# A second home for the mixer's mixed rows, and a layer norm moved within the mixer's loop

## The reference

```python
x = x + 0.5 * ffn(layernorm(x))        # shared expert + one of 8 routed experts per token
x = x + mixer(layernorm(x))
x = x + 0.5 * ffn(layernorm(x))

def mixer(x):
    u = x @ W_in + b_in                 # 256 -> 512 channels
    u = causal_conv4(u) + conv_b        # depthwise, 4 taps
    # per channel: h = tanh(A) h + u_t Bp ; y_t = Cp . h + D u_t   (16 states)
    y = silu(ssm(u))
    return y @ W_out + b_out            # 512 -> 256

def ffn(x):                             # swiglu: silu(x wg) * (x wu) @ wd
    return swiglu(x, shared) + swiglu(x * score, expert[argmax(x @ gate_w)])
```

## Time and profile before

| | |
|---|---|
| median of 3 runs | 890.16 us (887.72 to 890.94) |
| span of the profiled execution | 884.5 us |
| PE busy | 830.2 us, 94% of the span |
| VectorE busy | 489.0 us, 55% |
| ScalarE busy | 390.7 us, 44% |
| POOL busy | 459.1 us, 52% |
| mean granted TensorE clock | 0.991 of full |

### The profile page before, as it was taken

One profiled execution on the slowest core, in us unless ns is written; L12 is line 12 of the kernel. 1 busy time (PEld: TensorE's weight loads), 2 busy tenths in 40 slices (PEclk: granted clock), 3 DMA queues, 4 the chain that ended last, 5 costly groups with the idle time before them and its releaser, 6 DMA issues.

```text
span 884.5 us, 16195 instructions
## 1 busy us (share of the span) xinstructions
PE 830.2 (94%) x5302; PEld 720.8 (81%) x5303; DVE 489.0 (55%) x999; ACT 390.7 (44%) x766; POOL 459.1 (52%) x435
## 2 busy tenths in 40 slices
PE   5889999999999999989998999899999999999993
PEld 4677888888888878877887888688888888888883
DVE  7877843333333336678998886975433333333452
ACT  5633323334343434555786776223343434344330
POOL 6527850333334018869999982686330242330685
PEclk9999999999999999999999999999999999999997
DMA  7683443545564225331010014154335555421566
GB/s 262 241 326 104 170 161 114 202 174 213 167 218 157 74 88 80 43 44 17 13 54 26 25 50 191 48 183 179 110 127 194 197 194 195 167 89 30 108 155 154
DMA packets 52917, 118.15 MB, mean 134 GB/s; under 512 B 6426, under 2 KB 41380, under 8 KB 48516
## 3 DMA queue, kind: packets, MB, share of 16 engines
q0 software_dynamic: 17536, 74.33, 27.1%
q1 hardware_dynamic: 34834, 43.15, 14.8%
q10 hardware_dynamic: 498, 0.02, 0.0%
HBM read 83.25 MB, written 34.22 MB: 133 GB/s over the span
## 4 chain that ended last, share of the span: by engine, by line
PE 70%; POOL 13%; DVE 8%; issue 3%; DMA 3%; ACT 2%; POOLq 0%; DVEq 0%; ACTq 0%
PE bank L419 21%; PE bank L420 20%; PE bank L421 20%; POOL acc L1888 5%; PE bank L616 4%; DMA wr_hi<-w_routed 2%; PE bank L585 2%; POOL v L1791 2%; DVE v L1503 2%; POOL wr_lo L1858 1%; POOL yr L1997 1%; DVE xT_lo L1194 1%; PE bank L486 1%; POOL hT_lo L1795 1%; DMA xT_kept<-xTf_odd 1%
## 5 line engine op out<-in xcount | busy, mean ns | idle before, releaser
L1858 POOL TENSOR_TENSOR wr_lo<-wr_raw,wr_hi 128x3072 fp32r<-128x3072 f32 x14 | 95.4, 6812 | 105.3 <-DMA wr_hi<-w_routed 87.0
L419 PE MATMUL bank<-wr_hi,xT_hi 128*128 x312 | 130.1, 417 | 1.5 <-POOL wr_lo L1858 1.4
L420 PE MATMUL bank<-wr_hi,xT_lo 128*128 x312 | 123.8, 397 | 0.0
L421 PE MATMUL bank<-wr_lo,xT_hi 128*128 x312 | 122.9, 394 | 0.0
L1461 DVE TENSOR_TENSOR hf<-sg,bank 128x512 f32<-128x512 f32 x78 | 53.6, 688 | 125.2 <-PE bank L421 125.2
L1194 DVE TENSOR_TENSOR hT_lo<-bank,hT_hi 128x512 fp32r<-128x512 f32 x78 | 53.9, 691 | 124.6 <-ACT hT_hi L869 124.6
L1888 POOL DMA_INDIRECT acc<-ys_sorted,pos x52 | 84.7, 1628 | 54.3 <-DMA ys_sorted<-rows 39.9
L419 PE MATMUL bank<-xT_hi,ws_hi 128*128 128x512 f32 x256 | 103.1, 403 | 8.0 <-DVE hf L1299 5.5
L420 PE MATMUL bank<-xT_hi,ws_lo 128*128 128x512 f32 x256 | 101.3, 396 | 0.0
L421 PE MATMUL bank<-xT_lo,ws_hi 128*128 128x512 f32 x256 | 101.2, 395 | 0.0
L419 PE MATMUL bank<-wr_hi,hT_hi 128*128 x312 | 93.8, 300 | 3.0 <-DVE hT_lo L1194 3.0
(11 more groups left out here) (245 smaller groups left out, 2117.6 us busy)
## 6 DMA issues: line engine op xcount, KB each, us to landing
wr_raw<-w_routed POOLq DMA_DIRECT2D x16, 1536.0 KB, 7.0
wr_hi<-w_routed POOLq DMA_DIRECT2D x16, 1536.0 KB, 7.7
rows<-xs_sorted SPq DMA_DIRECT2D x78, 128.0 KB, 2.5
ys_sorted<-rows SPq DMA_DIRECT2D x78, 128.0 KB, 1.7
xg<-xT_kept SPq DMA_DIRECT2D x12, 512.0 KB, 5.5
xT_kept<-xTf SPq DMA_DIRECT2D x9, 512.0 KB, 2.6
acc<-x SPq DMA_DIRECT2D x8, 512.0 KB, 9.8
xs_sorted<-zeros POOLq DMA_DIRECT2D x4, 1024.0 KB, 11.6
```

The lines of the kernel that those rows point to most:

```text
L419: pe.matmul(o, a_hi, b_hi, start=start, stop=False, skip_group_check=True)
L420: pe.matmul(o, a_lo, b_hi, start=False, stop=False, skip_group_check=True)
L421: return pe.matmul(o, a_hi, b_lo, start=False, stop=stop, skip_group_check=True)
L1858: pool.tensor_tensor(wr_lo[:, e % 2, :], wr_raw[:, :], f32(wr_hi[:, e % 2, :]), ALU.subtract).then_inc(s_wl, 1)
```

## The change

Two tiles `xM_hi` and `xM_lo` are laid in the place of `rows`. `mix_hi`, `mix_lo` and `w_in_part` use them for odd groups and `xT_hi`, `xT_lo` for even ones; `mix_hi(n)` waits for the `w_in_part`s of group n-2 (for n = 1: for the stores of the routed rows of the first half). On ScalarE `ln2_apply(n+2)` moves from the middle of iteration n to its end, just ahead of `ln2_hi(n+2)`. On VectorE `ln2_stats(n+2)` moves from ahead of `taps(n-1, 2)` to behind `ln2_lo(n+1)`. POOL's and SyncE's programs stay as they are.

```diff
+        mixer_only = ExitStack()
+        xM_hi = sb("xM_hi", [P, KB, GN], F32R, mixer_only)
+        xM_lo = sb("xM_lo", [P, KB, GN], F32R, mixer_only)
+        mixer_only.close()
         rows = sb("rows", [P, 2 * GT, H], F32)
...
+        def mixed(n): return (xT_hi, xT_lo) if n % 2 == 0 else (xM_hi, xM_lo)
...
+                m_hi, m_lo = mixed(n)
                 for kb in range(KB):
-                    mm = mm3(pe, UB[cb % 2][:, :], win_hi[:, kb, cs], win_lo[:, kb, cs], xT_hi[:, kb, :],
-                             xT_lo[:, kb, :], start=(kb == 0), stop=(kb == KB - 1))
+                    mm = mm3(pe, UB[cb % 2][:, :], win_hi[:, kb, cs], win_lo[:, kb, cs], m_hi[:, kb, :],
+                             m_lo[:, kb, :], start=(kb == 0), stop=(kb == KB - 1))
...
             def mix_hi(n):
-                if n > 0:
-                    act.wait_ge(s_um, 4 * n)
+                if n == 1:
+                    for j in range(RING):
+                        act.wait_ge(s_yst[j], 16 * (NS // RING))
+                elif n > 1:
+                    act.wait_ge(s_um, 4 * (n - 1))
                 for kb in range(KB):
                     act.wait_ge(s_zp, KB * n + kb + 1)
-                    hi(xT_hi[:, kb, :], ZB[kb][:, :]).then_inc(s_zh, 1)
+                    hi(mixed(n)[0][:, kb, :], ZB[kb][:, :]).then_inc(s_zh, 1)
...
                     if live(n + 1):
                         state_hi(n + 1, 0)
-                    if live(n + 2):
-                        ln2_apply(n + 2)
                     if live(n - 1):
                         y_round(n - 1, 3)
...
                     if live(n - 2):
                         ln3_apply(n - 2)
                     if live(n + 2):
+                        ln2_apply(n + 2)
                         ln2_hi(n + 2)
...
-                    lo(xT_lo[:, kb, :], ZB[kb][:, :], xT_hi[:, kb, :]).then_inc(s_zl, 1)
+                    lo(mixed(n)[1][:, kb, :], ZB[kb][:, :], mixed(n)[0][:, kb, :]).then_inc(s_zl, 1)
...
                     if live(n - 3):
                         ln3_stats(n - 3)
-                    if live(n + 2) and n > 0:
-                        ln2_stats(n + 2)
                     if live(n - 1):
                         taps(n - 1, 2)
...
                     if live(n + 1) and n > 0:
                         ln2_lo(n + 1)
+                    if live(n + 2) and n > 0:
+                        ln2_stats(n + 2)
                     if live(n):
                         taps(n, 0)
                         taps(n, 1)
```

## The result

| | before | changed |
|---|---|---|
| median | 890.55 us (4 runs) | 911.39 us (4 runs) |
| ratio | 1 | 1.0245 (1.022 to 1.0269) |
| span of the profiled execution | 884.5 us | 908.6 us |
| mean granted TensorE clock | 0.991 | 0.987 |

A forecast was written before the change was run, and what follows sets the result against it. The prediction took POOL (GpSimd) to set the mixer loop's pace up to 480 us. Its terms, 0.6 + 5.8 + 3 x 4.7 less 0.6 us, gave +20 us on 890.16, so 910 us, range 902 to 919.

The forecast's parts named there:

- (a), the homes: Second home of the mixed rows: `mix_hi` waits less, pays once at the first handover, then PE's limit is `xl`.
- (b), the late apply: ScalarE's `ln2_apply` moved later: `ln2_lo` starts at t+9.6 instead of t+8.7, t being the start of `y_silu(n, 0)`.
- (c) and the sum: VectorE's `ln2_stats` moved behind `ln2_lo`: POOL waits at `ln2_rsqrt` anew each iteration; all parts total +20 us.
- up to t(1): Loop until `y_silu(1, 0)` starts: POOL's wait of 0 to 2.2 us, say 1.1, less 0.5 for collisions: +0.6 us.
- t(1) to t(2): From `y_silu(1, 0)` to `y_silu(2, 0)`: a stall of 6.8 us less 1.0 for collisions, +5.8 us.
- t(2) to t(5): From `y_silu(2, 0)` to `y_silu(5, 0)`: three iterations, each stretched 5.7 us less 1.0 for collisions, 3 x 4.7 us.
- given back behind t(5): After `y_silu(5, 0)` starts, PE takes over and `mix_chunk(7, 0)` can start relatively sooner; 0.6 us comes back.
- credit of 1 us per iteration: Taken off for n = 2 to 5, because a standing POOL no longer collides with `ln2_lo`: 1.0 us each.
- low bound of +15.4: Smallest loss: nothing at n = 1, statistics ending 1 us sooner each time, 4.9 + 3 x 3.7 - 0.6.
- Paid once: Rival: in the loop, work behind the stall catches up within the iteration; +5 to +13 us, 898 us, chance 0.10.
- Faster, and no change: Two rivals without POOL's stall: gaps close for -6 us, 884 us, chance 0.05; or nets out within 0.5%, chance 0.02.
- PE as the bound at the lower clock: Rival: in the loop, idle PE drops to half clock and becomes the bound; +28 to +45 us, 925 us, chance 0.07.

The follow-up runs named there:

- pool_busy: Kernel before with nothing moved, POOL filling an unused tile three times ahead of `ln2_rsqrt` in iterations 2 to 5; 906.8 us, ratio 1.0223.
- gather_only: Kernel before, one home, with two of the four gathers of group 3 set on POOL ahead of `add_bias(0, 0)`; 884.24 us, ratio 0.9955.
- homes_only: Changed kernel with `ln2_apply` and `ln2_stats` at their old places, so only the two homes of the mixed rows remain; 889.97 us, ratio 1.0016.
- front_loaded: Kernel before plus two homes, two gathers moved early, and `ln2_lo(1)`, `ln2_stats(3)`, `ln2_apply(2)` set ahead of the loop; 886.01 us, ratio 0.9968.
- front_one_home: `front_loaded` with a single home for the mixed rows; 885.53 us, ratio 0.9969.
- apply_back: Changed kernel with ScalarE's `ln2_apply(n+2)` put back behind `state_hi(n+1, 0)`; 907.7 us, ratio 1.0218.
- stats_back: Changed kernel with VectorE's `ln2_stats(n+2)` put back ahead of `taps(n-1, 2)`; 890.88 us, ratio 1.0026.
- one_late: Changed kernel with `ln2_stats(n+2)` late in iteration 2 alone and at its old place in the others; 896.23 us, ratio 1.0099.
- rsqrt_late: Changed kernel with POOL's `ln2_rsqrt(n+2)` moved behind `add_bias(n, 1)`; 893.26 us, ratio 1.0065.

## Why the prediction was right, point by point

**The bound.** POOL as the pace of the loop up to 480 us was the step that everything hung on. `pool_busy` and `gather_only` show it from both sides: 5.8 us of added POOL time per iteration cost 4.5 to 4.9 us each, and 3.55 us given back once moved t(5) by 3.65 us.

**(a), the homes.** Expected to pay only at the first handover and to run into `xl` there: `homes_only` is equal to before within its interval, and `front_loaded` against `front_one_home` shows the 0.9 us that two homes give at that gap and that none of it reaches the end.

**(b), the late apply.** `ln2_lo(4)`, ahead of the statistics that POOL waits for in iteration 3, was to start at t(2) + 9.6; it started at 449.66, t(2) + 9.74. Its share of the loop is what `apply_back` took away, 0.8 to 1.0 us in iterations 3 to 5 and nothing in iteration 2, as the sum has it. By itself (`stats_back`) it costs 2.3 us behind t(5). The sum had no term for that, and needed none while the stall was there: in the changed kernel `mix_chunk(7, 0)` starts at t(5) + 11.3, not + 14.6.

**(c) and the sum, term by term.** On the left is the forecast, on the right what the two traces show, with the 1.72 us by which the changed kernel's mixer starts late (386.49 against 384.77 us for the first instruction of the first `first_tap`) taken out. The row behind t(5) is read at the start of `mix_chunk(7, 0)`, 521.98 against 497.74 us:

| term | forecast | measured |
|---|---|---|
| up to t(1) | +0.6 | +2.2 |
| t(1) to t(2) | +5.8 | +6.1 |
| t(2) to t(5) | +14.1 | +14.6 |
| given back behind t(5) | -0.6 | -0.3 |
| sum | +20 (19.9) | +22.5 |
| outside the mixer | 0 | +1.7 |

The term that was mis-sized is the first. I had let `ln2_lo(2)` take 1.2 to 3.6 us and the wait 0 to 2.2; it took 4.34 us, and POOL waited 3.14 us. The collision there did not go away, it grew. The credit of 1 us per iteration for collisions that end was right: the `y_low` behind `ln2_rsqrt` took 1.30 us at 454.81 where the earlier trace rows had 2.35, and the steps grew by 4.8 to 4.9 us while POOL stood 6.04 to 6.06 us. The rule of the Trainium skill (SBUF — State Buffer, "Who interferes with whom"), that a VectorE instruction with two SBUF inputs and a GpSimd instruction that reads SBUF block each other, was weighed the right way here, except for the first term; how `ln2_lo(2)` came to wait so long is told below. The low bound of +15.4 has a slip, on which nothing hangs: for n = 2 `ln2_lo` had been taken at t + 8.7 already, so by its own terms it is 5.8 + 11.1 - 0.6 = +16.3.

The 1.7 us outside the mixer are a half-clock stretch that the profiled execution of the changed kernel has at about 50 us, where nothing was edited and the kernel before has none:

```profile
48.00:55.00 7.00, 5.81 (x47) 5.54 (x48) 4.82 (x13) 4.82 (x7) 0.00 (x0) 0.76 1.01 348
```

It explains 1.7 of the 3.3 us between the spans' difference of 24.1 us and the medians' of 20.8: one execution's share of it is chance. That 22.5 + 1.7 = 24.2 meets the 24.1 of the spans says that the terms are complete.

That the forecast of 910 us lies so near the median of 911.4 is in part luck. The span grew by 24.1 us where I had 20, and the distance from span to median, which I had kept at 5.7 us, was 2.8 in the changed kernel (911.4 - 908.6). My growth was 4.1 us too low and my distance 2.9 us too high, and they nearly cancel. The profiled execution of the kernel before was a fast one: in each run whose span is on record the time is about 1.9 us above the span, and by that its 884.5 us answer to 886.4, below all four timed runs (887.7 to 892.6).

**The rivals.** Paid once: `pool_busy` and the changed kernel itself pay in each iteration, and `one_late` shows that nothing of a stall is made up for, since 6.4 us stay up to t(5). Faster, and no change: the stall was there. PE as the bound at the lower clock: the granted clock was half in two stretches of the stage, after the 3.67 and the 1.98 us gap, and PE went on waiting after them; POOL's waits and the steps of iterations 4 and 5, without such a stretch, are as long as that of iteration 3. The Trainium skill (TensorE: Matmul & The Clock Gate, "What's actually happening") says that the throttled state is the default and that activity releases it. That thinned-out work would stay slow for longer was my reading of it, and the trace says otherwise. The windows from 450.9 to 522 us (PE busy 76 to 89%) show the full clock:

```profile
424.90:450.90 26.00, 20.17 (x122) 17.27 (x122) 16.77 (x37) 12.57 (x29) 18.93 (x28) 0.93 0.04 6
450.90:474.30 23.40, 19.59 (x138) 16.43 (x138) 16.96 (x37) 14.40 (x32) 16.34 (x24) 1.00 0.10 29
474.30:500.30 26.00, 19.82 (x139) 16.46 (x139) 16.96 (x37) 14.42 (x32) 18.92 (x28) 1.00 0.09 26
500.30:522.00 21.70, 19.26 (x139) 16.36 (x139) 17.16 (x37) 14.64 (x31) 18.90 (x27) 1.00 0.06 25
```

The columns are those of the earlier trace rows; each stretch runs from one `mix_chunk(n, 0)` to the next. PE's busy time of 19.3 to 20.2 us is above the 17.7 to 18.6 us there; why was not pursued.

**What I said the profile would show.** POOL's waits: five, the first short, yes; their sum of 28.3 us is above the 20 to 26 I gave, by the first one and by 0.2 to 0.3 us for each of the others. These are 6.0 to 7.0 us long; my "about 5" contradicted my own sum, which had 5.7 and 6.8. The steps: 24.95 and 23.38 us, where I had 24.7 and 23.1. PE's idle time: 26.4, not some 30 us. First gap about 1 us: 0.83.

## What to carry to other kernels

When a step moves to a later place in one engine's queue, look up every queue in which something waits for its result, the unedited ones first: here a 1.9 us step moved into a place after the point where POOL asked for it, and POOL's wait held up work that had nothing to do with it. A stall in the queue that sets the pace of a pipelined loop is paid anew in each iteration, less the collisions that it ends (here 4.8 to 4.9 of 6.0 us); compare the step's new end with the moment the consumer arrives, both counted from the same point of the iteration, and the product with the iterations is the answer. A gap on the busiest engine is worth closing only if the chain behind it is not set elsewhere: closing 0.8 to 1.7 of PE's 2.8 us gap was worth nothing that the runs could show, 3.6 us of POOL's idle time before the loop was worth 4 us.

## What the runs showed of the hardware

The subtraction that makes `xl` (VectorE, 128x1024, both inputs in SBUF) takes 1.2 us alone, and took 3.59, 4.34 and 6.77 us next to POOL's steps of group 0. In each of these cases it ended 1.1 us after POOL's last reading step in a row. POOL in the changed kernel:

```profile
399.88 1.86 POOL L1804 TENSOR_TENSOR hT_lo<-v,hT_hi 128x512 fp32r<-128x512 f32 x1
401.11 1.84 POOL L1800 TENSOR_TENSOR v<-v,cbs 128x512 f32<-128x512 f32 x1
```

and VectorE beside it:

```profile
399.71 4.34 DVE L1203 TENSOR_TENSOR xl<-xg,xh 128x1024 fp32r<-128x1024 f32 x1 [1.07 <-ACT xh L876]
```

POOL's run ends at 402.95, `xl` at 404.05. In `rsqrt_late` POOL's four steps end at 403.33 and `xl` at 404.43; in the kernel before the two steps end at 401.27 and `xl` at 402.36. So it did not wait for one instruction of POOL but for the whole run of them, and a longer run makes a longer wait. In the changed kernel `xl` has its record at 399.71, 0.17 us ahead of the first of these two steps, and still lost: a gather of POOL was under way then (398.90 for 1.54 us), so the starts of the two records alone do not tell who waits. In the other order, where POOL is between two steps and `xl` is first by 0.04 us (457.33 against 457.37), it keeps its 1.2 us and POOL's step pays 1.1 us once. I had expected one collision to cost one instruction's length.
